# Two cross-attention layers in one kernel: the work around the second attention, its queries and the order of the first stages are changed

## The reference

```python
x = x + _L0_xattn_ref(_layernorm(x), ctx_1024, ...)   # 16 heads of 16 columns
x = x + _L0_ffn_ref(_layernorm(x), ...)               # 16 experts, two per token
x = x + _L1_xattn_ref(_layernorm(x), ctx_1024, ...)   # 16 heads of 128 columns
x = x + _L1_ffn_ref(_layernorm(x), ...)               # ternary weights
```

```python
q = rmsnorm((hidden_states @ Wq).reshape(B, Sq, H, D), gq)
k = rmsnorm((encoder_hidden_states @ Wk).reshape(B, Skv, H, D), gk)
v = (encoder_hidden_states @ Wv).reshape(B, Skv, H, D)
attn = softmax(einsum('bqhd,bkhd->bhqk', q, k) * scale)
out = einsum('bhqk,bkhd->bqhd', attn, v).reshape(B, Sq, H * D) @ Wo
```

## Time and profile before

| | us |
|---|---|
| three runs | 2430.64, 2431.26 (median), 2435.33 |
| the profiled execution, its own time | 2432.28 |
| its span, first to last instruction | 2430.5 |
| busy: PE, DVE | 2136.2 (88%), 1759.2 (72%) |
| busy: POOL, ACT | 1268.2 (52%), 1182.8 (49%) |

### The profile page before, as it was taken

How to read it: one execution, slowest core, us unless ns; L and a number is a source line. 1 busy time by engine, 2 the same in 40 slices (tenths; PEclk the granted TensorE clock), 3 DMA queues, 4 the chain that set the end, 5 groups by cost and what they waited for, 6 DMA issues and landing times. The chain is left out here.

```text
span 2430.5 us, 46202 instructions
## 1 busy us (share of the span) xinstructions
PE 2136.2 (88%) x16568; PEld 1687.4 (69%) x16568; DVE 1759.2 (72%) x2225; ACT 1182.8 (49%) x2007; POOL 1268.2 (52%) x1004
## 2 busy tenths in 40 slices
PE   5999999999994479999999793967999999999665
PEld 4888787887882357777777451536999999998433
DVE  5888888888885566666663434959999999996157
...
GB/s 108 119 91 153 118 119 128 115 151 120 91 129 58 113 81 112 116 155 117 111 137 2 216 69 93 33 177 59 82 78 106 73 86 81 79 73 29 223 0 15
DMA packets 93580, 244.20 MB, mean 100 GB/s; under 512 B 19377, under 2 KB 65362, under 8 KB 84162
## 3 DMA queue, kind: packets, MB, share of 16 engines
...
...
## 5 line engine op out<-in xcount | busy, mean ns | idle before, releaser
L317 DVE TENSOR_REDUCE rk<-n_sq 128x1024 f32 (+2 forms) x384 | 465.7, 1213 | 129.2 <-ACT n_sq L255 126.5
L1140 POOL TENSOR_TENSOR a_S<-a_S,a_mb 128x896 f32<-128x896 f32 x192 | 513.9, 2713 | 27.5 <-ACT a_mb L1168 27.5
L255 ACT ACTIVATE n_sq<-n_slot 128x1024 f32<-128x1024 f32 (+1 forms) x384 | 394.3, 1027 | 140.3 <-PE n_slot L211 131.9
L1174 ACT ACTIVATE a_S<-a_S 128x896 f32<-128x896 f32 x192 | 182.9, 953 | 331.1 <-POOL a_S L1140 331.1
L209 PE MATMUL n_slot<-n_wh,n_yh 128*128 128x512 f32 (+1 forms) x768 | 318.5, 415 | 25.4 <-POOL n_yl L153 25.4
L993 PEld LDWEIGHTS a_ob<-a_y,a_S 128*128 128x128 f32 (+1 forms) x2688 | 324.4, 191 | 8.3 <-issue 2.2
L993 PE MATMUL a_ob<-a_y,a_S 128*128 128x129 f32 (+1 forms) x2688 | 327.7, 275 | 2.3 <-issue 1.7
L1478 DVE TENSOR_REDUCE a_mpart<-a_pre 112x2 f32<-112x1024 f32 (+1 forms) x192 | 218.8, 1184 | 117.6 <-PE a_pre L1316 117.6
L211 PE MATMUL n_slot<-n_wh,n_yl 128*128 128x512 f32 (+1 forms) x768 | 303.7, 395 | 0.0
L210 PE MATMUL n_slot<-n_wl,n_yh 128*128 128x512 f32 (+1 forms) x768 | 302.0, 393 | 0.0
L1414 ACT ACTIVATE a_pr<-a_sc 128x448 f32<-128x448 f32 (+1 forms) x384 | 205.2, 545 | 190.4 <-PE a_sc L1345 178.0
...
## 6 DMA issues: line engine op xcount, KB each, us to landing
...
```

Source lines behind the costliest of these rows:

```text
L255: act.activation(sq[0:n, w, :], slot[w][0:n, :], ACT.Square).then_inc(slot_free, 1)
L317: dve.tensor_reduce(g.rk[0:n, b, j, 8 * s:8 * s + 8], sq[0:n, (2 * j + s) % 3, :].rearrange("p (h d) -> p h d", h=8), X, ALU.add)\
L1140: pool.tensor_tensor(S[1 - i][0:n, j, :], S[1 - i][0:n, j, :], mb[0:n, :], ALU.subtract)\
L1174: act.activation(S[1 - i][0:n, j, :], S[1 - i][0:n, j, :], ACT.Exp).then_inc(p_ready, 1)
```

## The change

- **Order of the first stages.** Layer norm l0 and `phase_queries0` now come before `phase_keys`. The loads and splits with which the keys began (`load_splits`, `split_context`, `high_weights`, `split_first_weights`, `split_weights`) are put into `phase_queries0`.
- **Queries of the second attention.** The unit is now 112 tokens (on the partitions) and four heads (512 columns): 32 units, four chunks of heads. All products have high and low parts. Squares on ACT, sum along the row, reciprocal and product on DVE, then four transposes per unit on PE (`turn`), high part on ACT and low part on DVE, and per head and half the product with the key weights (`back`, 32 pieces, 12 steps behind). Weights are split by POOL, the first chunk already beside the layer norm. Eight transfers store two heads each from two buffers; the phase no longer waits for them.
- **Ends of the second attention.** The split queries of batch 0 are left in SBUF by the queries, so that PE needs no load. For the last batches DVE takes two chunks of batch 14 and seven of batch 15 from POOL. M is made in steps 16 (PE `weights`, ACT copies), its weights loaded during the attention, and the first half of `ot` is loaded before the phase ends.
- **`phase_project1`** begins with the products.

```diff
+def load_splits(sp, g):
+    sp.dma_start(g.yT[0][:, :], g.a["ctxT"][0]).then_inc(g.yT_in[0], 16)
+    sp.dma_start(g.wkv[:, 0:D], g.a["L0_Wk"]).then_inc(g.w0_in, 16)
+    sp.dma_start(g.wkv[:, D:2 * D], g.a["L0_Wv"]).then_inc(g.w0_in, 16)
+    sp.dma_start(g.kbias[:, :], g.a["bk0"]).then_inc(g.w0_in, 16)
+    sp.dma_start(g.wall[:, :], g.a["L1_Wk"]).then_inc(g.w1_in, 16)
+    sp.dma_start(g.yT[1][:, :], g.a["ctxT"][1]).then_inc(g.yT_in[1], 16)
...
+def split_context(pool, g):
+    pool.wait_ge(g.yT_in[0], 16)
+    pool.tensor_tensor(g.yh[0][:, :], g.yT[0][:, :], g.ones[:, 0:1].broadcast_to([P, SEQ]), ALU.mult).then_inc(g.y_high, 1)
+    pool.wait_ge(g.y_high, 1)
+    pool.tensor_tensor(g.yl[0][:, :], g.yT[0][:, :], g.yh[0][:, :], ALU.subtract).then_inc(g.y_split, 1)
+def high_weights(act, g):
+    act.wait_ge(g.w1_in, 16)
+    act.activation(g.wh[:, :], g.wall[:, :], ACT.Copy).then_inc(g.w1_high, 1)
+def split_first_weights(dve, g):
+    by_head = lambda t: t.rearrange("p (h d) -> p h d", h=H)
+    dve.wait_ge(g.w0_in, 48)
...
+    dve.tensor_copy(g.kvh[:, :], g.wkv[:, :]).then_inc(g.w0_steps, 1)
+    dve.wait_ge(g.w0_steps, 5)
+    dve.tensor_tensor(g.kvl[:, :], g.wkv[:, :], g.kvh[:, :], ALU.subtract).then_inc(g.w_split, 1)
+def split_weights(dve, g):
+    dve.wait_ge(g.w1_high, 1)
+    dve.tensor_tensor(g.wl[:, :], g.wall[:, :], g.wh[:, :], ALU.subtract).then_inc(g.w_split, 1)
...
             pool.memset(rs[:, :, :], 1.0).then_inc(set_up, 1)
-            high_y(0, 0, 0)
-            low_y(0, 0)
-            pool.wait_ge(set_up, 5)
-            pool.wait_ge(w0_steps, 5)
+            pool.wait_ge(set_up, 6)
...
                 dve.tensor_copy(v2(qc[half]), ps[2 + half][:, :, 0:HALF]).then_inc(c_ready, 1)
+            split_first_weights(dve, g)
             for half in range(2):
                 dve.wait_ge(rooted, half + 1)
...
+def split_wq(pool, g, c):
+    w, high, low = g.wq[c % 2][:, :, :], g.wqh[c % 2][:, :, :], g.wql[c % 2][:, :, :]
+    pool.wait_ge(g.wq_in[c % 2], 16 * (c // 2) + 16)
+    pool.tensor_tensor(high, w, g.ones[:, 0:1].unsqueeze(1).broadcast_to([P, 2, HC * HD1]), ALU.mult).then_inc(g.wq_high, 1)
+    pool.wait_ge(g.wq_high, c + 1)
+    pool.tensor_tensor(low, w, high, ALU.subtract).then_inc(g.wq_split, 1)
...
+            def project(u):
+                c, t = u // NT, u % NT
+                if t == 0:
+                    pe.wait_ge(g.wq_split, c + 1)
+                if c == 0 and t % 4 == 0:
+                    pe.wait_ge(x_split, t // 4 + 1)
+                if u >= 4:
+                    pe.wait_ge(q_normed, u - 3)
+                cols = slice(t * TT, (t + 1) * TT)
+                for k in range(2):
+                    high, low = xh[:, k, cols], xl[:, k, cols]
+                    pe.matmul(pq[u % 4][0:TT, :], high, g.wqh[c % 2][:, k, :], start=(k == 0), stop=False)
+                    pe.matmul(pq[u % 4][0:TT, :], high, g.wql[c % 2][:, k, :], start=False, stop=False)
+                    mm = pe.matmul(pq[u % 4][0:TT, :], low, g.wqh[c % 2][:, k, :], start=False, stop=(k == 1))
+                mm.then_inc(q_psum, 1)
+            def turn(u):
+                pe.wait_ge(q_normed, u + 1)
+                if u >= 2:
+                    pe.wait_ge(q_low, u - 1)
+                for h in range(HC):
+                    mm = pe.transpose(tp[u % 2][:, h * TT:(h + 1) * TT], qn[u % 4][:, h * HD1:(h + 1) * HD1],
+                                      g.ident[0:TT, 0:TT])
+                mm.then_inc(qT_psum, 1)
+            def back(v, c, h, half):
+                if v % NT == 0:
+                    pe.wait_ge(wk_split, c + 1)
+                    pe.wait_ge(q_low, NT * (c + 1))
+                if v >= 2:
+                    pe.wait_ge(copied, v - 1)
+                high, low = v2(qh[c % 2], half)[:, h, :], v2(ql[c % 2], half)[:, h, :]
+                dst = po[v % 2][:, 0:HALF]
+                pe.matmul(dst, wkh[c % 2][:, h, :], high, start=True, stop=False)
+                pe.matmul(dst, wkh[c % 2][:, h, :], low, start=False, stop=False)
+                pe.matmul(dst, wkl[c % 2][:, h, :], high, start=False, stop=True).then_inc(out_psum, 1)
+            for u in range(UNITS + BACK):
+                if u < UNITS:
+                    project(u)
+                if 0 <= u - TR < UNITS:
+                    turn(u - TR)
+                if piece(u):
+                    back(*piece(u))
...
+            def square(u):
+                act.wait_ge(q_psum, u + 1)
+                if u >= 2:
+                    act.wait_ge(summed, u - 1)
+                act.activation(sq[u % 2][:, :], pq[u % 4][0:TT, :], ACT.Square).then_inc(squared, 1)
+            def root(u):
+                act.wait_ge(summed, u + 1)
+                act.activation(ss[:, u % 4, :], ss[:, u % 4, :], ACT.Sqrt, scale=1.0 / HD1, bias=eps[0:TT, 0:1])\
+                   .then_inc(rooted, 1)
+            def high(u):
+                c, t = u // NT, u % NT
+                act.wait_ge(qT_psum, u + 1)
+                if t == 0 and c >= 2:
+                    act.wait_ge(out_psum, NT * (c - 1))
+                act.activation(qh[c % 2][:, :, t * TT:(t + 1) * TT],
+                               tp[u % 2][:, 0:HC * TT].rearrange("p (h n) -> p h n", h=HC), ACT.Copy).then_inc(q_high, 1)
+            def out(v, c, h, half):
+                n, side = v // 4, h % 2
+                act.wait_ge(out_psum, v + 1)
+                if v % 4 == 0 and n >= 2:
+                    act.wait_ge(g.q_stored[n % 2], 16 * (n // 2))
+                    act.wait_ge(q0_split, n - 1)
+                act.activation(qo[n % 2][:, 8 * half:8 * half + 8, side * NQ:(side + 1) * NQ],
+                               po[v % 2][:, 0:HALF].rearrange("p (b q) -> p b q", q=NQ), ACT.Copy).then_inc(copied, 1)
+                if v % 4 == 3:
+                    act.wait_ge(copied, v)
+                    act.activation(g.Qh[:, 2 * NQ * n:2 * NQ * (n + 1)], qo[n % 2][:, 0, :], ACT.Copy).then_inc(q0_high, 1)
...
+            def sums(u):
+                dve.wait_ge(squared, u + 1)
+                if u >= 4:
+                    dve.wait_ge(q_normed, u - 3)
+                dve.tensor_reduce(ss[:, u % 4, :], by_head(sq[u % 2][:, :]), X, ALU.add).then_inc(summed, 1)
+            def normalise(u):
+                dve.wait_ge(rooted, u + 1)
+                dve.reciprocal(ss[:, u % 4, :], ss[:, u % 4, :]).then_inc(inverted, 1)
+                dve.wait_ge(inverted, u + 1)
+                if u >= 4:
+                    dve.wait_ge(qT_psum, u - 3)
+                dve.tensor_tensor(by_head(qn[u % 4]), by_head(pq[u % 4][0:TT, :]),
+                                  ss[:, u % 4, :].unsqueeze(2).broadcast_to([TT, HC, HD1]), ALU.mult).then_inc(q_normed, 1)
+            def low(u):
+                c, t = u // NT, u % NT
+                dve.wait_ge(q_high, u + 1)
+                cols = slice(t * TT, (t + 1) * TT)
+                dve.tensor_tensor(ql[c % 2][:, :, cols], tp[u % 2][:, 0:HC * TT].rearrange("p (h n) -> p h n", h=HC),
+                                  qh[c % 2][:, :, cols], ALU.subtract).then_inc(q_low, 1)
...
+    DVE_END = (10, 11)
+    DVE_LAST = (0, 2, 3, 5, 7, 8, 10)
+    NM = H // 2
...
-            load_queries(0, 0)
+            for i in range(2):
+                sp.wait_ge(g.q_stored[i], 8 * NG)
...
+            sp.wait_ge(stored, 16 * (B // 2))
+            sp.dma_start(g.ot0, od[0:B // 2].rearrange("b c n -> c b n")).then_inc(g.ot0_in, 16)
...
+                def weights(lo, hi):
+                    for m in range(lo, hi):
+                        if m == 0:
+                            pe.wait_ge(g.wo_in, 16)
+                            pe.wait_ge(g.wv_in, 16)
+                            pe.wait_ge(s_scaled, SC * B)
+                        if m >= 2:
+                            pe.wait_ge(m_copied, m - 1)
+                        for k in range(2):
+                            mm = pe.matmul(ring[m % 2][:, k * D:(k + 1) * D], g.wv[:, 2 * m + k, :], g.M[:, 2 * m + k, :],
+                                           start=True, stop=True)
+                        mm.then_inc(m_psum, 1)
...
+                    if last and j == 2:
+                        weights(0, 3)
                     if back and j == 2:
                         spread()
+                    if last and j == LAG:
+                        weights(3, NM)
...
+                if last:
+                    shift(B - 2, i, DVE_END[0], mb)
                 for j in range(NK):
                     n = rows(j)
+                    if last and j == 2:
+                        shift(B - 2, i, DVE_END[1], mb)
+                        dve.wait_ge(mb_ready, 2 * B)
+                    if last and j >= 2:
+                        for k in DVE_LAST[0:2] if j == 2 else DVE_LAST[2:] if j == LAG + 1 else ():
+                            shift(B - 1, 1 - i, k, Q)
...
+                if last:
+                    act.wait_ge(q_split, B)
+                    weights(0, 3)
...
```

(29 more changed lines are left out.)

427 lines of the change are left out of this document (222 added, 205 removed).

## The result

The changed kernel takes 2379.66 us in the median of four runs (2378.42 to 2381.09), the kernel before 2433.05 in four (2430.64 to 2435.33). The ratio is 0.9781, its 95% interval 0.9764 to 0.9798. Forecast were 2378 and a range of 2360 to 2396. The profiled execution has a span of 2378.2, 52.3 less than before, and a mean PE clock of 0.935 (0.928). In the later runs the kernel before took 2430.3 to 2431.5 in the median, which would make the gain 51 to 52. All runs of this document ran at nearly the same granted clock except one of experiment 2's four (2535.14 us at a clock of 0.809), which is left out.

A forecast was written before the change was run, and what follows sets the result against it. Long engines stood still at three joints; PE bound the second attention's queries. 13.6 + 25.0 - 5.2 + 19.4 = 52.8 off 2432.28 gave 2379.5, less 1.0 for the median: 2378 us, range 2360 to 2396.

The forecast's parts named there:

- The start: Program start to dca: 16.7 us removed, less 2.8 for splits in queries0 and 0.3 in the keys; gain 13.6, 11 to 16.
- the row of 4.77: Start: DVE's large subtraction took 4.77 us beside POOL; taken as covered by the stores, uncovered costing up to 4.8.
- The layer norm: Layer norm before the second attention's queries: DVE slower beside POOL's splits of the first weights; loss 1 us, 0 to 3.
- The queries: Second attention's queries, to DVE's first scaled score: 105.3 us instead of 131.3; gain 26.0, less 1 for the layer norm.
- The loop of waits: Queries: with two transpose banks, `turn` waits for `low` two units back; 2.8 us per step, 2.5 in steps 4 to 11.
- The end of the attention: Second attention's end: M's products and copies delay batch 15's exponentials, then PE is the bound; loss 5.2 us, 0 to 9.
- Project1: Project1: 22.4 us of loading and making M removed, 3.0 lost to PE's half clock; gain 19.4, 17 to 22.
- the term for the clock: Project1: PE starts at half clock after its pause, 6.0 us at half, so 3.0 lost.
- the loop is closed: Queries: the rival denied this, with PE's 2.4 (2.2 without back) ruling; 10 us less, 2368; chance 0.20.
- it alone keeps the step above PE's own 2.4: Queries: the rival claimed more waits than seen, 3.3 us per step, 14 more, 2392; chance 0.17.
- The late loads: Rival: project1 or the last step waits for `ot` or M's weights; up to 10 us of gain missing, 2388; chance 0.05.
- PE's clock was at 1.00: Queries: the rival claimed PE's clock stays at half, 4.8 us per step, 60 more, 2438; chance 0.03.

The follow-up runs named there:

- experiment 2: Changed kernel with M made again in project1, its weights and all stored outputs loaded there, and POOL alone shifting the last chunks: 2396.48 us, ratio 0.9852.
- experiment 1: Kernel before with only the new start: layer norm l0 and queries0 ahead of the keys, splits inside queries0: 2417.13 us, ratio 0.9943.
- experiment 3: Changed kernel with three PSUM banks for the queries' transposes and three for the projections, instead of two and four: 2370.43 us, ratio 0.9751.
- Experiment 7: Changed kernel with the last five of M's eight pairs placed between the output products of batch 15: 2378.47 us, ratio 0.9787.
- experiment 12: Changed kernel without M's eight pairs of products and their copies, part of the computation left out: 2371.27 us, ratio 0.9753.
- experiment 6: Changed kernel with all twelve shifts of the last batch on POOL again, DVE keeping only two of batch 14: 2378.66 us, ratio 0.9781.
- experiment 8: Changed kernel with 24 additional PE products that nobody reads, to keep PE busy before project1: 2373.92 us, ratio 0.976.

## Why the prediction was right

**The start** was mis-sized, by 2.5. The block of the keys shrank by 17.5, not by 16.7 less 0.3. PE's clock rose 2.3 us sooner in it; at half clock half of that is lost, so about 1.1 of the difference, an estimate that no run takes apart. The splits cost 2.2 (57.4 to 59.6 from l0 to the keys), not 2.8. The remaining 0.8 is the setup, which ended that much earlier in this execution. In experiment 1 it didn't; there the splits cost 1.3 (58.8 from l0 to the keys), and the gain at dca was again 16.1, but 14.2 by the medians. The choice of the row of 4.77 for the large subtraction was harmless, as it was covered.

**The layer norm** was the weakest term: 1 taken, 3.2 measured, above my upper bound of 3. The step that failed is the price of POOL beside DVE. I had read the 4.77 for 2048 columns as "somewhat slower". POOL's row beside it in the timeline of the kernel before, which I didn't use, says more:

```profile
17.27 2.69 POOL L148 TENSOR_TENSOR n_yh<-n_yT,ones 128x1500 fp32r<-128x1500 f32 x1 [1.60 <-DMA n_yT<-in_ctxT]
```

DVE's subtraction started at 17.34, stood until POOL was done at 19.96, 2.6, and took 2.15 more, about the 2.28 that it takes now by itself. Such a DVE operation stands until POOL's is over. The Trainium skill says this in SBUF — State Buffer, Who interferes with whom, of DVE instructions with two SBUF inputs beside a GpSimd instruction that reads SBUF, and of the 2-port modes that `copy`, `cast` and `tensor_scalar` can enter: whoever issues first gets the shared pair of ports for the whole instruction, and the other fully blocks. The two long ones of the eight, 1.56 and 2.50 against 0.40, agree. So do the shifts of the last batches, in the same view of two lines of the changed kernel (`p_S` are DVE's two for batch 14, with POOL idle; `a_S` those of batch 15, on both engines at once):

```profile
L1259 DVE TENSOR_TENSOR a_S<-a_S,a_Q x7: 1079/2964/2979, 2195.4 to 2210.9; 128x896 f32<-128x896 f32 x7
L1259 DVE TENSOR_TENSOR p_S<-p_S,a_mb x2: 1077/1078/1080, 2185.2 to 2189.5; 128x896 f32<-128x896 f32 x1, 92x896 f32<-92x896 f32 x1
```

```profile
L1348 POOL TENSOR_TENSOR a_S<-a_S,a_Q x5: 2924/2940/2985, 2195.4 to 2207.1; 128x896 f32<-128x896 f32 x4, 92x896 f32<-92x896 f32 x1
```

The long ones take their own time and the other's: 1.08 + 2.05 = 3.1, and 2.96 is measured. Not every DVE operation stands. These three divisions, whose first source is in PSUM, ran beside POOL's second shift and took 1.22, as the three at the end do, when POOL is idle:

```profile
2199.84 1.22 DVE L1269 TENSOR_TENSOR a_on<-a_ob,a_rden 128x384 f32<-128x384 f32 x3
```

Had I reckoned that a subtraction stands until POOL is done, I would have charged POOL's two splits, 4.2 us as an estimate (1.89 + 2.34), less what of them falls beside no subtraction.

**The queries.** The loop of waits was the forecast's core, and it is there: 2.71 per step for 2.8, and experiment 3 removes it. The schedule held up to the sixth group's last copy: PE's start at 2.2 (2.2 forecast), step 4 at 10.9 (11.0), step 12 at 30.5 (31), step 32 at 86.4 (87), that copy at 92.7 (92). Mis-sized was what follows. The store lasted 7.1 us, until 1582.58, and not 5.5, with another store behind it; the last four pieces took 3.8 and not 2.3, PE being at half clock after its wait; the last store 4.8. Together 3.1 late. Windows in this stretch show 276 GB/s while a store runs (rows below), so the 269 of the earlier trace rows was about the right rate. The 341 of the Trainium skill's DMA: Bandwidth & Descriptors, Bandwidth, is measured there for loads from HBM to SBUF; these stores in pieces of 448 bytes don't reach it, and it would have shortened a term that came out too short.

**The end of the attention** came out at 5.2 for 5.2, and the order of events was as written (spread 7.8 after the last maximum, forecast 7.3; first exponential 19.2, forecast 18.9; PE without a pause after it). But the reason that I gave, exponentials standing behind M's copies, isn't what it costs, and that the number came out is in part luck. Experiment 7 took them from behind the copies and won 0.1; experiment 12 shows the price, 7.5, of which PE's own eight times 0.86 make 6.9. Without M the shifts on DVE are worth 2.3, and 7.5 less 2.3 is the 5.2; but beside M the seven of the last batch are worth nothing (experiment 6), and what the two of batch 14 are worth there no run shows. The sum also has the five pairs at 4.3, which is 0.215 per record and not the 0.28 that stands before it; they took 4.67 (row of 2199.30).

**Project1**: 19.6 for 19.4, and the term for the clock 2.8 for 3.0, shown by experiment 8. The 24.32 for the first half before the change doesn't stand in the earlier trace rows, whose row ends after 36 of the 64 products; the whole trace has it.

None of the rivals was right. That the loop is closed, and that it alone keeps the step above PE's own 2.4, is shown by the run with three banks. The late loads didn't show: `ot` and M's weights were there when used. PE's clock was at 1.00 from 1495 to 1565.
